# A vision tower on one NeuronCore: where the layer weights are loaded and fused, and the order in which slices, peaks, planes and gates stand in the plan

## Chip, cores, metric

The kernel runs on one core of one Trainium2 chip. The metric is the device time of one execution in microseconds (us), as the median of the runs of one kernel on one chip.

## What is computed

The reference, cut to its steps, with B = 64 images of 12 channels and 224 x 224 pixels, 196 tokens, width 192 and 4 experts:

```python
pooled = x.reshape(B, 12, 14, 16, 14, 16).sum(axis=(3, 5))
h = einsum('bcij,ce->bije', pooled, channel_weights).reshape(B, 196, 192)
n = layernorm(h); Q, K, V = n@Wq.T + bq, n@Wk.T + bk, n@Wv.T + bv
h = h + softmax(Q @ K.T / sqrt(192)) @ V
x = layernorm(h); probs = softmax(x @ w_router.T)
gate, idx = top_k(swapaxes(probs, 1, 2), 98)       # each expert takes 98 of 196 tokens
y = layernorm(x) * gamma1 + beta1
h = sum over experts of dispatch(mask(y[idx])) @ w1.T + b1
x_mlp, q, k, v = split(h)                          # 768, and 12 heads of 16
y2 = concat([gelu(x_mlp), softmax(q @ k.T / 4) @ v])
z = sum over experts of gate * mask(y2[idx] @ w2.T + b2)
out = h_tokens + x + z[..., :192] + z[..., 192:]
```

## The kernel before

Since the tokens are linear in 12 channel sums, the first attention works on 12 to 14 numbers per token, and U = 104 columns carry what the experts chose. The 64 images are taken in 8 groups of 8.

**Pooling.** Per pair of images, three tiles of x of 1568 KB (`xt`, three buffers, `fetch` issues the next load from the ACT queue, L1109) are summed by DVE in 7 slices (`pool`, L1256), GpSimd spreads them (`own_row`, L1576), TensorE turns them (`planes`, L830), ACT copies, TensorE makes token values (`tok`, L840), DVE copies (L1269). A group has four such pairs (m = 0 to 3).

**Routing** of a group, a chain: `take`, `norm1_scale`, `norm1`, first attention (`first_max`, `first_exp`, `first_mix`), `stream` to `stream_norm`, then `gate_scale` (L1354), a power on GpSimd (L1585, about 2.9 us), `gate_logits` (L1360), again a power, `gates` (L1373), `gate_rows` (L920, L1385), 13 rounds of `choose` on DVE (L1393, L1398), `chosen` (L928, L1411), `spread` (L1421), and `turn_u` (L936).

**Second attention and MLP** of an image: `project` (L968, low halves on DVE at L1445), through a scratch in DRAM to `stack`, `peak` (a score block, L986, whose row maximum DVE takes at L1456), `shift` (the 12 maxima turned at L995, copied by ACT, sent by a small DMA from SP, L730, as one more row of `qs`), `score` (L1005, exponential at L1205), `mix` (L1020), `hidden` (L956, GELU at L1183), `fc2` (L1051). `score` of heads 0 to 5 waits for the first shift row, of heads 6 to 11 for the second.

**The order** is a plan written by hand. `body` gives a group 8 x 12 slots (image, head), each with the peak of the next image's head, the score of this one, and what `fill`, `routing`, `choosing`, `turning` and `pooling` put there; every engine runs the same list in order. The plan ends with the `opening` of the next group: 8 steps with one `hidden` each, the twelve peaks of its image 0, and the tail of the last image. In pass g the slots also hold the routing of group g + 1 from slot `TAKE` on, the last pair of group g + 1, and pairs 0 to 2 of group g + 2. The sections are `prologue` (all of group 0 up to its opening, and pairs 0 to 2 of group 1), six passes `loop`, then `pen` (no pairs for a group after the next) and `last`. A slot of a plan is a place in the list, not a time.

**Setup.** SP loads the attention weights, `G` and small vectors, then w1 and w2 (L688 to L692, 2.4 MB), tile 3, and, once ACT has copied `Vp`, the product of channel and value weights, out of PSUM (L1077), a DMA that puts it into rows 12 to 23 of `G` (L696). DVE waits for this DMA before it centres `G` (L1520). `fuse` turns w1 and w2 (L814) and multiplies them into `M` (L821, L823) in three parts, at slots inside the pooling of pairs 1 to 3; part 0 on DVE adds the halves of w2 (L1264). The line that places them, and the four PSUM buffers:

```python
front += [(pieces * (m + 1) + 4, ("fuse", 0, m)) for m in range(3)]
MISC = 4
```

In the opening `hidden` and `project` share these four buffers; a buffer that held q or k is free when DVE has taken its low half (L1450).

## Time and profile before

| | before |
|---|---|
| median of 3 runs | 1775.73 us (1774.58 to 1777.63) |
| the profiled execution | 1772.98 us, its span 1771.2 us |
| TensorE matmuls (PE) | 1519.9 us, 86% of the span |
| VectorE (DVE) | 1218.1 us, 69% |
| ScalarE (ACT) | 848.6 us, 48% |
| GpSimd (POOL) | 249.4 us, 14% |
| mean granted TensorE clock | 0.921 |
| first score of groups 0 to 7, at | 231.8, 437.2, 637.5, 839.0, 1040.1, 1242.6, 1447.8, 1629.2 us |

The profiled execution is 2.75 us below the median. Spans are in us from the first instruction. PEclk is the granted TensorE clock, 1.00 for 2.4 GHz and 0.50 for 1.2 GHz. A loop pass takes 200 to 205 us, six of them make up two thirds of the span.

### The profile page before, as it was taken

The numbers are of one execution on the slowest core, as the hardware profiler recorded it, in microseconds if no ns is written. First come the engines' busy times: TensorE is split into PE (matmuls) and PEld (weight loads), VectorE is DVE, ScalarE is ACT, GpSimd is POOL, SyncE is SP. The second block draws the span as 40 slices with busy tenths as digits, with TensorE's granted clock in tenths as the row PEclk, the third lists the DMA queues.
The fourth block names the chain that finished last, engine by engine and source line by source line (L and its number), as shares of the span: only waits on it lengthen the run. The fifth ranks groups of instructions, "written<-read, shape, count | busy, mean of one in ns | idle before, by whom it ended". The sixth has DMA issues, their size and how long they took to land.

```text
span 1771.2 us, 34644 instructions
## 1 busy us (share of the span) xinstructions
PE 1519.9 (86%) x12440; PEld 1260.6 (71%) x12440; DVE 1218.1 (69%) x2822; ACT 848.6 (48%) x1935; POOL 249.4 (14%) x318
## 2 busy tenths in 40 slices
PE   1364689998998899989998899999899889989998
PEld 1233567777786777778787777778677778878786
DVE  3847678766887578865887568875787567563552
ACT  0101355545554555545654554545554555546654
POOL 2012002200121002200121002210022002110000
PEclk9757689989999999999999989989998899989999
DMA  9867376706573357606664356615656151102220
GB/s 225 233 166 195 89 179 158 188 15 161 148 187 99 85 148 178 184 16 158 156 168 117 76 145 168 180 40 136 165 149 148 35 145 45 42 19 59 50 53 15
DMA packets 99598, 218.03 MB, mean 123 GB/s; under 512 B 61371, under 2 KB 75877, under 8 KB 88678
## 3 DMA queue, kind: packets, MB, share of 16 engines
q10 hardware_dynamic: 11904, 149.33, 31.3%
q1 hardware_dynamic: 87526, 66.49, 16.5%
q8 instruction: 102, 1.67, 0.4%
q14 instruction: 66, 0.54, 0.1%
HBM read 186.57 MB, written 28.90 MB: 122 GB/s over the span
## 4 chain that ended last, share of the span: by engine, by line
PE 50%; DVE 25%; issue 13%; DMA 5%; POOL 3%; ACT 2%; SPq 1%; DVEq 0%; ACTq 0%; POOLq 0%
PE bank L1051 13%; DVE psums L1256 10%; DVE peaks L1456 6%; PE bank L956 6%; PE bank L986 5%; PE bank L1020 5%; PE bank L1005 4%; DMA qs<-shiftT 3%; POOL var L1585 3%; PE bank L968 2%; PE bank L879 2%; PE bank L830 2%; PE bank L1029 2%; PE bank L943 2%; DVE qk L1445 1%
## 5 line engine op out<-in xcount | busy, mean ns | idle before, releaser
L1456 DVE TENSOR_REDUCE peaks<-bank 98x2 f32<-98x392 f32 x768 | 423.6, 563 | 170.3 <-PE bank L986 149.3
L1205 ACT ACTIVATE Pb<-bank 98x392 f32<-98x392 f32 x768 | 374.9, 497 | 300.1 <-PE bank L1005 250.9
L1256 DVE TENSOR_REDUCE psums<-xt 112x2 f32<-112x512 f32 x672 | 425.7, 677 | 27.1 <-DVE peaks L1456 9.7
L1051 PE MATMUL bank<-w2T,hid 128*98 128x192 f32 x1536 | 311.4, 342 | 0.0
L986 PE MATMUL bank<-ks,qs 96*98 96x196 f16 x1536 | 268.4, 261 | 42.8 <-DVE peaks L1456 37.9
L1005 PE MATMUL bank<-qs,ks 97*98 97x196 f16 x1536 | 268.3, 258 | 22.1 <-DMA qs<-shiftT 20.2
L986 PEld LDWEIGHTS bank<-ks,qs 96*98 96x98 f16 x1536 | 165.5, 128 | 132.7 <-DVE peaks L1456 66.2
L1051 PEld LDWEIGHTS bank<-w2T,hid 128*98 128x98 f32 x1536 | 249.5, 176 | 3.5
L1005 PEld LDWEIGHTS bank<-qs,ks 97*98 97x98 f16 x1536 | 167.3, 130 | 34.5 <-DMA qs<-shiftT 22.9
L1020 PE MATMUL bank<-Pb,vals 98*32 98x196 f32 x3072 | 171.9, 342 | 1.2 <-ACT Pb L1205 1.2
L1613 POOL TENSOR_TENSOR fin<-fin,both 98x384 f32<-98x384 f32 x64 | 63.9, 999 | 732.9 <-DVE fin L1481 732.9
L956 PE MATMUL bank<-UT,M 104*128 104x196 f32 x768 | 150.8, 347 | 16.9 <-DVEq L1450 16.9
L956 PEld LDWEIGHTS bank<-UT,M 104*128 104x128 f32 x768 | 133.7, 200 | 21.8 <-DVEq L1450 19.3
L1183 ACT ACTIVATE hid<-bank 128x392 f32<-128x392 f32 x192 | 93.5, 497 | 109.9 <-PE bank L956 109.7
L1445 DVE TENSOR_TENSOR qk<-bank,qk 96x392 f16<-96x392 f32 x128 | 71.7, 560 | 84.6 <-ACT qk L1192 74.6
L1576 POOL TENSOR_TENSOR spread_p<-psums,cst 112x196 f32<-112x196 f32 x96 | 50.0, 521 | 533.2 <-DVE psums L1256 533.2
L1020 PEld LDWEIGHTS bank<-Pb,vals 98*32 98x32 f32 x3072 | 81.3, 110 | 54.2 <-issue 25.0
L1117 ACT COPY oT<-bank 128x196 f32<-128x196 f32 x192 | 61.9, 322 | 106.8 <-PE bank L1020 102.4
L1051 PE MATMUL bank<-w2T,onT 96*98 96x192 f32 (+1 forms) x512 | 108.3, 334 | 0.0
L968 PE MATMUL bank<-UT,M 104*96 104x196 f32 x512 | 99.0, 337 | 0.1
L830 PE MATMUL bank<-spread_p,cst 112*24 112x196 f32 x192 | 44.4, 376 | 48.8 <-POOL spread_p L1576 43.3
L1585 POOL TENSOR_TENSOR var<-var,cst 98x16 f32<-98x16 f32 x24 | 69.7, 2904 | 106.7 <-DVE var L1289 58.7
(183 smaller groups left out, 1783.6 us busy)
## 6 DMA issues: line engine op xcount, KB each, us to landing
xt<-in_x_dram ACTq DMA_DIRECT2D x93, 1568.0 KB, 9.0
qk_scratch<-qk SPq DMA_DIRECT2D x64, 294.0 KB, 4.1
qs<-qk_scratch SPq DMA_DIRECT2D x192, 73.5 KB, 3.0
ks<-qk_scratch SPq DMA_DIRECT2D x192, 73.5 KB, 3.1
out_dram<-fin SPq DMA_DIRECT2D x64, 147.0 KB
xt<-in_x_dram SPq DMA_DIRECT2D x3, 1568.0 KB, 8.8
qs<-shiftT SPq DMA_DIRECT2D x128, 2.3 KB
hid<-in_L_ffn_w_dram SPq DMA_DIRECT2D x1, 1440.0 KB
```

The source lines that it names most:

```text
L956: mm = pe.matmul(ps[:, T * j:T * j + T], M[:, 128 * f:128 * f + 128], UT[:, i, :], start=True, stop=True)
L968: mm = pe.matmul(ps[0:DC, T * c:T * c + T], M[:, f:f + DC], UT[:, i, :], start=True, stop=True)
L986: mm = pe.matmul(peak_ps[s][0:HT, T * q:T * q + T], qs[0:KS, i % NSTACK, h, HT * q:HT * q + HT], ks[0:KS, i % NSTACK, h, :], start=True, s ...
L1005: mm = pe.matmul(score_ps[s][0:HT, T * k:T * k + T], ks[:, i % NSTACK, h, HT * k:HT * k + HT], qs[:, i % NSTACK, h, :], start=True, stop=True)
L1020: mm = pe.matmul(ps[32 * j:32 * j + 32, 0:T], vals[:, i % 2, q, h, :], Pb[:, (H * i + h) % NP, q, :], start=(q == 0), stop=(q == 1))
L1051: mm = pe.matmul(misc_ps[slot][0:HT, D * h:D * h + D], lhs, w2T[0:w, f, :], start=(f == 0), stop=(f == NF + 1))
L1183: act.activation(hid[:, i, 2 * b:2 * b + 2, :].rearrange("p a b -> p (a b)"), ps[:, 0:2 * T], ACT.Gelu).then_inc(free, 1)
L1205: act.activation(Pb[:, (H * i + h) % NP, :, :].rearrange("p a b -> p (a b)"), score_ps[s][0:HT, 0:2 * T], ACT.Exp, scale=float(DH) ** -0.5 ...
L1256: last = dve.tensor_reduce(psums[:, m % 2, t, 2 * p:2 * p + 2], v[:, 2 * p:2 * p + 2, :, :], AX.XY, ALU.add)
L1445: dve.tensor_tensor(qk16[:, m, 1, :, :].rearrange("p c t -> p (c t)"), misc_ps[slot][0:DC, 0:2 * T], qk16[:, m, 0, :, :].rearrange("p c t ...
L1456: dve.tensor_reduce(peaks[:, h // 6, :, h % 6], peak_ps[s][0:HT, 0:2 * T].rearrange("p (q k) -> p q k", q=2), AX.X, ALU.max, negate=True). ...
L1585: gp.tensor_tensor(var[:, 2, :], var[:, 1, :], const("half", HT), ALU.pow).then_inc(gp_pow, 1)
```

## The change

It moves work in the plan and in the queues, and takes out one DMA; the sums and products are the same.

1. w1, w2, b1, b2 are loaded when 11 of group 0's 12 tiles are pooled. Tile 3 is fetched from the ACT queue.
2. `Vp` and its DMA are gone: `cwcT` has 25 columns, zero but for the middle 12, so that the product lands in rows 12 to 23 of PSUM and DVE adds it to `G`, which GpSimd has zeroed.
3. `fuse` 0, 1, 2 stand in group 0's routing: after `stream_norm`, between `gate_logits` and `gates`, and after the first `choose`. `L` moves into `UT`. Planes and tok of pair (1, 1) stand behind `spread`.
4. Opening: peaks of heads 0, 1 in step 2 in place of 1, and so on; 10 and 11 in step 7; the first shift in step 6, the second at the end. Slices of the opening stand ahead of its peaks. Planes and tok of the last pair there go to slots 2 and 4 of the next pass; for the two pairs before, planes stand 5 slots behind the last slice, in place of 3.5.
5. `TAKE` 23 in place of 25, `gate_logits` 3 slots behind `gate_scale` and `gates` 4 behind that (2 and 3 before); `gate_rows` stays in its slot, `chosen` comes a slot later. The slices of pair (1, 3) have 19 slots in place of 21.

```diff
 
-def routing(dg, at):
+def routing(dg, at, wide=0):
@@ -192,9 +192,9 @@
...
     at += 14
-    ops += [(at, ("gate_scale", dg)), (at + 2, ("gate_logits", dg)), (at + 5, ("gates", dg)),
-            (at + 7, ("gate_rows", dg)), (at + 7.5, ("weigh", dg))]
-    at += 8
+    ops += [(at, ("gate_scale", dg)), (at + 2 + wide / 2, ("gate_logits", dg)), (at + 5 + wide, ("gates", dg)),
+            (at + 7 + wide, ("gate_rows", dg)), (at + 7.5 + wide, ("weigh", dg))]
+    at += 8 + wide
@@ -227,16 +227,19 @@
...
-    front += [(pieces * (m + 1) + 4, ("fuse", 0, m)) for m in range(3)]
...
     front += first + [(at + 0.5 * r, ("choose", 0, r)) for r in range(ROUNDS)]
+    front += [(end + 34.5, ("fuse", 0, 0)), (at - 4.5, ("fuse", 0, 1)), (at + 0.2, ("fuse", 0, 2))]
     front += choosing(0, at + 0.5 * ROUNDS + 1)
     front += pooling(1, 0, steadily(end + 9, 0.95))
-    front += pooling(1, 1, steadily(end + 29, 0.65))
+    late = pooling(1, 1, steadily(end + 29, 0.65))
+    front += [(at + 0.5 * ROUNDS + 1.7 + 0.5 * (op[0] == "tok") if op[0] in ("planes", "tok") else slot, op)
+              for slot, op in late]
     plan = [in_order(front + turning(0, at + 0.5 * ROUNDS + 3))] + opening(0, False)
-    for slot, op in in_slots(pooling(1, 2, steadily(1, 0.24))):
-        plan[min(slot, len(plan) - 1)].append(op)
+    for slot, op in in_slots(pooling(1, AHEAD - 1, steadily(1, 0.24))):
+        if op[0] not in ("planes", "tok"):
+            plan[min(slot, len(plan) - 1)].append(op)
@@ -266,16 +269,16 @@
...
-        if 1 <= i < 7:
-            ops += [("peak", dg, 0, h) for h in range(2 * (i - 1), 2 * (i - 1) + 2)]
-        if i == 5:
+        if i >= 2:
+            ops += [("peak", dg, 0, h) for h in range(2 * (i - 2), 2 * (i - 2) + 2)]
+        if i == 6:
             ops.append(("shift", dg, 0, 0))
     ops.append(("shift", dg, 0, 1))
...
-TAKE = 25
+TAKE = 23
@@ -326,24 +329,28 @@
...
-    front, at = routing(1, TAKE)
+    front, at = routing(1, TAKE, 2)
...
     quiet = (int(at), H * GRP)
     at = rounds(plan, 1, int(at))
-    for slot, op in in_slots(choosing(1, at + 1) + turning(1, at + 4)):
+    for slot, op in in_slots(choosing(1, at + 2) + turning(1, at + 4.5)):
         plan[slot].append(op)
...
     at = evenly(plan, pieces * (GRP // PAIR - AHEAD), 0, TAKE - 4)
-    front = []
+    front = [(2, ("planes", 1, AHEAD - 1)), (4, ("tok", 1, AHEAD - 1))]
...
         at = evenly(plan, pieces * AHEAD, TAKE + 1, len(plan) - 3, quiet)
         for m in range(AHEAD):
-            front += pooling(2, m, at[pieces * m:])
+            front += pooling(2, m, at[pieces * m:], behind=5)
     for slot, op in in_slots(front):
-        plan[min(slot, len(plan) - 1)].append(op)
+        if op[0] in ("planes", "tok") and op[1:] == (2, AHEAD - 1):
+            continue
+        into = plan[min(slot, len(plan) - 1)]
+        peaks_at = [k for k, other in enumerate(into) if other[0] == "peak"]
+        into.insert(peaks_at[0] if slot >= H * GRP and peaks_at else len(into), op)
     return sum(plan, [])
@@ -517,7 +524,6 @@
...
-        cwcT = sb("cwcT", [DC, 2, C])
+        cwcT = sb("cwcT", [DC, 2, Z])
...
-        L = P1[0:DC, :, :, :].rearrange("p a b c -> p (a b c)")[:, 0:2 * U].rearrange("p (c e z) -> p c e z", c=2, e=E)
+        L = UT[0:DC, :, :].rearrange("p i t -> p (i t)")[:, 3 * 2 * D:3 * 2 * D + 2 * U].rearrange("p (c e z) -> p c e z", c=2, e=E)
...
         turns.append(([(wr_in[:, DC * c:DC * c + DC], E * c, E, DC) for c in range(2)],
...
+                      cwcT[:, :, C:2 * C]))
@@ -674,29 +680,27 @@
...
-            sp.dma_start(G[0:C, :], cw).then_inc(w_in, 16)
-            sp.dma_start(G[2 * C:Z, :], bv.rearrange("(a d) -> a d", a=1)).then_inc(w_in, 16)
...
                         .then_inc(w_in, 16)
+            sp.wait_ge(g_zero, 1)
+            sp.dma_start(G[0:C, :], cw).then_inc(w_in, 16)
+            sp.dma_start(G[2 * C:Z, :], bv.rearrange("(a d) -> a d", a=1)).then_inc(w_in, 16)
...
+            for t in range(NX + 1, NX + SETUP_TILES):
+                sp.wait_ge(pooled, t - NX + 1)
+                sp.dma_start(xt[:, t % NX, :], x_tile(0, t)).then_inc(x_in[t % NX], 16)
+            sp.wait_ge(pooled, TILES * GRP // PAIR - 1)
             sp.dma_start(w1_in[:, 0:10, :], w1[0:1280, :].rearrange("(f p) d -> p f d", p=128)).then_inc(w12_in, 16)
...
             sp.dma_start(b2_in[:, 0:2, :], b2.rearrange("(a o f) -> a o f", a=1, o=2)).then_inc(w12_in, 16)
-            sp.wait_ge(pooled, 1)
-            sp.dma_start(xt[:, 0, :], x_tile(0, NX)).then_inc(x_in[0], 16)
-            sp.wait_ge(su_act, 2)
-            sp.dma_start(G[C:2 * C, :], Vp).then_inc(su_dma, 16)
-            for t in range(NX + 1, NX + SETUP_TILES):
-                sp.wait_ge(pooled, t - NX + 1)
-                sp.dma_start(xt[:, t % NX, :], x_tile(0, t)).then_inc(x_in[t % NX], 16)
@@ -756,11 +760,11 @@
...
                     for d in range(2):
-                        mm = pe.matmul(banks[1][0:C, 0:D], cwcT[:, d, :], wa_T[:, 2, d, :],
+                        mm = pe.matmul(banks[1][0:Z, 0:D], cwcT[:, d, :], wa_T[:, 2, d, :],
@@ -1068,17 +1072,20 @@
             act.wait_ge(w_in, 16 * W_LOADS)
             for t in range(1, NX):
                 act.dma_start(xt[:, t, :], x_tile(0, t)).then_inc(x_in[t], 16)
+            act.wait_ge(pooled, 1)
+            act.dma_start(xt[:, 0, :], x_tile(0, NX)).then_inc(x_in[0], 16)
             for n_, (parts, dst) in enumerate(turns):
                 if n_ == NT - 1:
                     act.wait_ge(su_pe, 1)
...
-                    act.wait_ge(su_pe, 2)
-                    act.copy(Vp, banks[1][0:C, 0:D]).then_inc(su_act, 1)
@@ -1494,6 +1501,7 @@
...
+            dve.memset(cwcT[:, :, :], 0.0)
@@ -1516,7 +1524,8 @@
...
-            dve.wait_ge(su_dma, 16)
+            dve.wait_ge(su_pe, 2)
+            done(dve.tensor_tensor(G, G, banks[1][0:Z, 0:D], ALU.add))
@@ -1562,6 +1571,7 @@
...
+            gp.memset(G, 0.0).then_inc(g_zero, 1)
```

Left out are the plain consequences (a semaphore for the zeroed `G`, counts of waits).

**Group 0's choosing rounds, PE.** Before (`L920` gate rows, `L830` and `L840` the pair (1, 1), `L928` the choice turned):

```order
55 L912 MATMUL bank<-WR,zT 98x148 x2
56 L920 MATMUL bank<-cst,prob 32x98 x2
57 L830 MATMUL bank<-spread_p,cst 24x196 x3
58 L840 MATMUL bank<-WI,planesT 98x48 x2
59 L928 MATMUL bank<-cst,rows 98x32 x2
```

With the change (`L818` the turns of w1 and w2, `L924` gate rows, `L825` and `L827` the products into `M`):

```order
46 L818 MATMUL bank<-cst,both 128x96 x12
47 L818 MATMUL bank<-cst,both 96x96 x4
48 L924 MATMUL bank<-cst,prob 32x98 x2
49 L825 MATMUL bank<-hid,UT 104x384 x2
50 L827 MATMUL bank<-M,cst 104x384
...
55 L825 MATMUL bank<-hid,UT 104x192 x2
56 L827 MATMUL bank<-M,cst 104x192
57 L932 MATMUL bank<-cst,rows 98x32 x2
58 L834 MATMUL bank<-spread_p,cst 24x196 x3
59 L844 MATMUL bank<-WI,planesT 98x48 x2
```

The products stand between gate rows and the choice, the pair behind it.

**The opening in a loop pass, ACT.** Before (`L1183` GELUs, three to an image, `L1109` fetches, `L1117` copies of shift row and planes):

```order
238 L1109 DMA xt<-in_x_dram 112x3584
239 L1183 ACTIVATE hid<-bank 128x392 x3
240 L1117 CAST shiftT<-bank 6x196
241 L1183 ACTIVATE hid<-bank 128x392 x3
242 L1109 DMA xt<-in_x_dram 112x3584
243 L1183 ACTIVATE hid<-bank 128x392 x3
244 L1117 CAST shiftT<-bank 6x196
245 L1117 COPY planesT<-bank 24x196
```

With the change (lines are 7 higher):

```order
242 L1116 DMA xt<-in_x_dram 112x3584
243 L1190 ACTIVATE hid<-bank 128x392 x6
244 L1116 DMA xt<-in_x_dram 112x3584
245 L1124 CAST shiftT<-bank 6x196
246 L1190 ACTIVATE hid<-bank 128x392 x3
247 L1124 CAST shiftT<-bank 6x196
```

The first shift row stood six GELUs ahead of the planes' copy and ahead of the last fetch; it now stands right behind that fetch.

**The same opening, DVE.** Before (`L1456` peaks, `L1256` slices, `L1445` low halves), then with the change (`L1463`, `L1263`, `L1452`):

```order
648 L1456 TENSOR_REDUCE peaks<-bank 98x2 x2
649 L1256 TENSOR_REDUCE psums<-xt 112x2 x2
650 L1456 TENSOR_REDUCE peaks<-bank 98x2 x2
651 L1256 TENSOR_REDUCE psums<-xt 112x2 x5
652 L1445 TENSOR_TENSOR qk<-bank,qk 96x392 x2
```

```order
646 L1263 TENSOR_REDUCE psums<-xt 112x2 x7
647 L1463 TENSOR_REDUCE peaks<-bank 98x2 x2
648 L1452 TENSOR_TENSOR qk<-bank,qk 96x392 x2
649 L1263 TENSOR_REDUCE psums<-xt 112x2 x4
650 L1463 TENSOR_REDUCE peaks<-bank 98x2 x2
```

Five slices stood ahead of the low halves; now two peaks do.

## Rows read from the trace of the kernel before

**Rows 1.** Busy time by stretch, one loop period: us, then busy per engine, PEclk, DMA share, GB/s
```profile
783.00:984.00 201.00, 184.18 (x1540) 154.12 (x1540) 149.61 (x348) 104.67 (x240) 29.63 (x39) 0.95 0.52 133
```

**Rows 2.** Timeline of DVE, start of the program: start us, length, line, idle before and its releaser
```profile
42.36 0.34 DVE L1520 TENSOR_REDUCE mean<-hid 25x1 f32<-25x192 f32 x1 [26.91 <-DMA hid<-hid]
...
83.64 4.24 DVE L1256 TENSOR_REDUCE psums<-xt 112x2 f32<-112x512 f32 x7 [2.57 <-DMA xt<-in_x_dram]
89.93 4.24 DVE L1256 TENSOR_REDUCE psums<-xt 112x2 f32<-112x512 f32 x7 [2.04 <-DMA xt<-in_x_dram]
...
106.86 0.26 DVE L1269 COPY tok_raw<-bank 98x96 f32<-98x96 f32 x1 [9.71 <-PE bank L840]
107.04 7.20 DVE L1256 TENSOR_REDUCE psums<-xt 112x2 f32<-112x512 f32 x12
...
118.79 0.26 DVE L1276 COPY wtok<-tok_raw 98x192 f32<-98x192 f32 x1
```

**Rows 3.** DMA issues of the page, tiles of x: count, KB each, us to landing
```profile
xt<-in_x_dram ACTq DMA_DIRECT2D x93, 1568.0 KB, 9.0
```

**Rows 4.** Busy time by stretch, at the start
```profile
20.00:30.00 10.00, 2.23 (x10) 1.15 (x9) 0.00 (x0) 0.50 (x2) 0.00 (x0) 1.00 1.05 269
...
90.00:100.00 10.00, 10.00 (x16) 3.35 (x15) 5.45 (x9) 0.31 (x1) 0.52 (x1) 0.50 0.74 209
```

**Rows 5.** Timeline of DVE at the start, the sum of the two halves of w2
```profile
58.47 2.14 DVE L1264 TENSOR_TENSOR both<-hid 96x1920 f32<-96x1920 f32 x1
```

**Rows 6.** Timeline of PE, group 0's fused weights and its choosing rounds
```profile
90.69 2.88 PE L821 MATMUL bank<-hid,P 96*104 96x384 f32 x4
...
106.05 0.78 PE L840 MATMUL bank<-WI,planesT 24*98 24x48 f32 x4
...
172.09 0.48 PE L920 MATMUL bank<-cst,prob 98*32 98x98 f32 x2 [12.16 <-DVEq L1380]
174.65 2.12 PE L830 MATMUL bank<-spread_p,cst 112*24 112x196 f32 x6 [2.08 <-POOL spread_p L1576]
177.27 0.86 PE L840 MATMUL bank<-WI,planesT 24*98 24x48 f32 x4 [0.49 <-ACT planesT L1117]
189.29 0.34 PE L928 MATMUL bank<-cst,rows 32*98 32x32 f32 x2 [11.16 <-issue]
```

**Rows 7.** Timeline of PE, opening of a later group
```profile
817.77 2.98 PE L956 MATMUL bank<-UT,M 104*128 104x196 f32 x8 [2.46 <-DVEq L1450]
...
836.64 1.18 PE L830 MATMUL bank<-spread_p,cst 112*24 112x196 f32 x6
...
838.96 0.33 PE L1005 MATMUL bank<-qs,ks 97*98 97x196 f16 x2
```

**Rows 8.** Busy time by stretch, around that opening's stall and after the gates
```profile
750.00:756.00 6.00, 6.00 (x26) 5.40 (x26) 4.21 (x12) 0.99 (x2) 1.92 (x1) 0.51 0.73 154
...
815.00:824.00 9.00, 6.54 (x22) 5.76 (x22) 3.22 (x6) 1.66 (x4) 0.52 (x1) 0.63 0.54 139
```

**Rows 9.** Timeline of PE, image 5 of the same loop pass
```profile
742.69 0.37 PE L1005 MATMUL bank<-qs,ks 97*98 97x196 f16 x2 [1.69 <-DMA qs<-shiftT]
...
747.68 1.16 PE L830 MATMUL bank<-spread_p,cst 112*24 112x196 f32 x6 [2.10 <-POOL spread_p L1576]
```

**Rows 10.** Timeline of POOL, the same place
```profile
744.14 2.91 POOL L1585 TENSOR_TENSOR var<-var,cst 98x16 f32<-98x16 f32 x1 [4.75 <-DVE var L1354]
```

**Rows 11.** Timeline of ACT, two issues of a tile of x
```profile
734.30 0.32 ACTq L1109 DMA_DIRECT2D xt<-in_x_dram  x1
...
833.00 0.32 ACTq L1109 DMA_DIRECT2D xt<-in_x_dram  x1
```

**Rows 12.** Timeline of SP, a shift row's issue
```profile
735.38 0.68 SPq L730 DMA_DIRECT2D qs<-shiftT  x1
```

**Rows 13.** Timeline of PE, before the choice of rows is turned
```profile
785.99 0.25 PE L928 MATMUL bank<-cst,rows 32*98 32x32 f32 x2 [3.11 <-issue]
```

**Rows 14.** Timeline of PE, group 6, before its gates
```profile
1546.73 0.37 PE L986 MATMUL bank<-ks,qs 96*98 96x196 f16 x2 [1.37 <-DVE peaks L1456]
```

More of the change, by code:

```diff
@@ L519, in bass_vit_tower @@
         Gc = scratch(Z, D)
-        Vp = scratch(C, D)
         w2_sum = both[0:DC, 0:2 * (HID + D)] \
@@ L550, in bass_vit_tower @@
         turn_full, turn_free = sem("turn_full"), sem("turn_free")
-        su_dve, su_pe, su_act, su_dma = sem("su_dve"), sem("su_pe"), sem("su_act"), sem("su_dma")
+        su_dve, su_pe, su_act, g_zero = sem("su_dve"), sem("su_pe"), sem("su_act"), sem("g_zero")
         bias_in = sem("bias_in")
@@ L648, in bass_vit_tower @@
         turns.append(([(cwc[:, DC * c:DC * c + DC], C * c, C, DC) for c in range(2)],
-                      cwcT[:, :, :].rearrange("p c e -> p (c e)")))
+                      cwcT[:, :, C:2 * C]))
         turns.append(([(Gc[:, DC * c:DC * c + DC], Z * c, Z, DC) for c in range(2)],
@@ L758, in _ @@
                                 mm = pe.matmul(banks[0][0:DC, 12 * (2 * m + c):12 * (2 * m + c) + 12],
-                                               wa_T[:, m, d, DC * c:DC * c + DC], cwcT[:, d, :],
+                                               wa_T[:, m, d, DC * c:DC * c + DC], cwcT[:, d, C:2 * C],
                                                start=(d == 0), stop=(d == 1))
@@ L948, in hidden @@
                 if at.section == "pro":
-                    pe.wait_ge(su_act, 3)
+                    pe.wait_ge(su_act, 2)
                     pe.wait_ge(bias_in, 16)
@@ L961, in project @@
                 if at.section == "pro":
-                    pe.wait_ge(su_act, 3)
+                    pe.wait_ge(su_act, 2)
                 pe.wait_ge(UT_ready, GRP * G_ + i + 1)
@@ L1080, in _ @@
                 cols = parts[-1][1] + parts[-1][2]
-                act.copy(dst, misc_ps[n_ % MISC][0:rows_, 0:cols]).then_inc(turn_free, 1)
+                src = misc_ps[n_ % MISC][0:rows_, 0:cols]
+                if len(dst.shape) == 3:
+                    src = src.rearrange("p (c e) -> p c e", c=2)
+                act.copy(dst, src).then_inc(turn_free, 1)
             def fuse(at, G_, dg, part):
```

## The prediction

> **What bounds the kernel now.** I read the busy time of a loop period first, then the timelines. Over one period of 201 us PE is busy 184.18 us and DVE 149.61 us [rows 1]: TensorE carries the time, and what a pass can lose is its 16.8 us idle and what it does at half rate. So the loop's price is read at each place where PE waits, and the start, where DVE and the loads set the pace, is read apart.
>
> At the start DVE stands still for 26.91 us until a 9 KB DMA lands [rows 2]: it is queued with 2.4 MB of w1 and w2, and between 20 and 30 us the DMA engines are full although no slice runs [rows 4]. Later slices wait for tiles that come 6.29 us apart (83.64 to 89.93), then 9.71 us for a `tok` that sits behind the products into `M`, and the last slice ends at 107.04 + 7.20 = 114.24 [rows 2].
>
> In a loop pass there are four larger waits. (a) In the opening PE waits 2.46 us for DVE's low halves of image 2 [rows 7], which stand behind five slices; after it the clock is down (0.63 granted over 9 us, so 6.7 us at 1.2 GHz) [rows 8]. (b) At image 5, 1.69 us for a shift row, whose DMA was issued right behind a tile of x. (c) Then 2.10 us for a spread slice [rows 9] that GpSimd does behind the 2.91 us power of the gates [rows 10]; here too 6 us at half rate follow, PE being busy for all of it [rows 8]. (d) 3.11 us before the choice [rows 13], where DVE ends its rounds.
>
> **The start, step by step.** The DMA into `G` and its wait go; DVE goes on when the product is in PSUM, about 22 us. Tile 1 is issued at 14.6 as before, and a tile takes 9.0 us to land [rows 3]: 23.6. Ten more at 6.2 us (nearest: 6.29) put tile 11 at 85.6; its slices end 4.24 us later, at 89.8 [rows 2]. That is 24.4 us before 114.24. The ends: 26 if tiles come 6.0 us apart; 15 if the 2.4 MB, released when tile 10 is pooled, go wholly ahead of tile 11 (about 9 us at the 269 GB/s of [rows 4]). I take 24.4, since tile 11 is then all but landed.
>
> Moved into the routing: the addition of w2's halves, 2.14 us [rows 5] and 0.3 us for b2's, stands on DVE in a stretch where DVE has slices back to back: +2.4 us on the path. The turns of w1 and w2 fall into PE's 12.16 us of idle before gate rows [rows 6]: nothing, and about 2 us if that cover were gone. The products took from 90.69 to 106.05, 15.4 us, at half rate although PE was busy all the time [rows 4, 6]. They now start at gate rows and must end by the choice: 189.29 - 172.09 = 17.2 us [rows 6]. They just fit: nothing, and 1 to 3 us late if copies or the choice are earlier. Planes and tok of pair (1, 1), 177.27 + 0.86 - 174.65 = 3.5 us [rows 6], move out of that cover behind `spread`, whose 2.1 us and PE's own 3.0 us of waiting cover all but 0.5. Group 0's opening I leave as it is: its slices still stand behind the peaks. Start: 24.4 - 2.4 - 0.5 = **21.5 us** gained.
>
> **The loop, per pass.**
> - Opening, the stall (a). Two peaks stand ahead of the low halves now, not five slices: 2.46 us gone, and with it 6.7 us at half rate, of which 6.3 busy: 3.1 us. Back comes a wait of peaks 6, 7 behind the last slices and `gate8` on DVE, 0.8 us by their durations. So the last fetch, behind the GELUs of image 6, is issued at 833.00 - 4.8 = 828.2 [rows 11].
> - The shift row. It is now sent right behind this fetch. At (b) the same happened: fetch 734.30, shift row 735.38, score 742.69, that is 8.39 us from the fetch to the score [rows 9, 11, 12]. So the first score comes at 828.2 + 8.4 = 836.6, where it came at 838.96 [rows 7]: 2.4 us gained of the 4.8 plus the 2.1 us of planes and tok that left (836.64 to the next peak). PE would be there at about 832.3 and waits some 4 us.
> - Planes and tok come back in slots 2 and 4 of the next pass, 1.18 us [rows 7] and about 0.5: -1.6. DVE has two more slices in the first image: -0.3.
> - Gates (c). The power starts two slots earlier against PE's planes, and 3 slots are more than its 2.91 us: 2.10 us of wait and half of 6 us at the low clock: **5.1 us**, the largest term. Bounds: 0 if the spread is still late, 5.1.
> - Waits for shift rows. The fetch ahead of (b) stands a slot earlier: +1.3 of 1.69. Two fetches now stand a slot ahead of second shift rows (images 3 and 4), where none did: up to -1.69 each by the same row; slots there are long, I take -1.0 in all.
> - Choice (d). PE has one slot more of work in front of it: +0.9 of 3.11.
>
> Sum: 2.4 - 1.6 - 0.3 + 5.1 + 1.3 - 1.0 + 0.9 = **6.8 us** a pass, 41 us in six. In `pen` the power delays the peaks by 1.37 us [rows 14]: 1.4 + 0.9 = 2.3.
>
> The profiled execution is 1772.98 us: 1772.98 - 21.5 - 41 - 2.3 = 1708. The median of the runs is 2.75 us higher, so I forecast **1711 us**, against 1775.73.
>
> The shift row is where a page rule is weighed. The row shows a small DMA, alone in its queue, that releases PE 8.39 us after the tile's issue, about when a tile lands [rows 3, 9, 11]. The Trainium skill (DMA: Bandwidth & Descriptors, Queues, rings and completion order) says the semaphore increment "lands only after every earlier write from that SDMA engine, across its queues", which speaks against this change; the trace agrees at (b). The same section says that an engine takes turns between its queues packet by packet; by that alone the row would overtake the tile, and rival 1 below would hold.
>
> **Rivals.**
> 1. *The small DMA is early.* The first score then starts when PE is there, 832.3 and not 836.6: 4.3 us more a pass, 26 in all, 1685. For it: the fetch could slip behind the shift row if ACT's GELUs run late. Against: (b) shows 8.39 us, and the order on ACT puts the fetch first.
> 2. *The loop keeps its waits under other names.* The planes no longer wait for GpSimd, but the clock is still down after the shift wait or after DVE's peaks, and the first image, with DVE and PE both nearly full, pays 2 us. Then a pass gains 2.3: 1773.0 - 21.5 - 14 - 1 = 1736.5, as a median 1739. For it: a pass has many small waits on peaks, and each could grow when its neighbour shrinks. Against: PE is idle 16.8 us of 201 [rows 1] and the two stalls are single events with a cause.
> 3. *The start gives little,* because w1 and w2 hold up the tiles after all or the products do not fit under the choosing rounds: 10 us in place of 21.5, 1722.
> 4. *Slower: the opening's shift wait.* Place: the first score of each pass. If (a) stays, the fetch is at 833.0 and lands after 9.8 us: score at 842.8, 3.9 us late. The idle PE then runs 6 us at half rate (3.0), planes and tok cost 1.6, the two new neighbours 3.4, and only 5.1 + 1.3 + 0.9 come in: 4.6 us lost a pass. With 27.6 lost in six and 23.8 gained elsewhere: 1777 against 1773, 1780 as a median. It decides from about 4 us a pass. For it: a wait of about 4 us is sure in my own sum. Against: it needs (a) too, which five slices in front of one low half made. The skill's page on TensorE (TensorE: Matmul & The Clock Gate, What's actually happening) says that idleness returns the array to half rate and activity lifts it; (c) shows both.
>
> **How the numbers follow.** Forecast 0.50, rival 1 0.15, rival 2 0.24, rival 3 0.06, rival 4 0.05. The forecast's own range is 1698 to 1725: 4 us of the start, 1.5 us a pass. Range: rival 1's 1688 as a median below, rival 2's 1739 above. A difference of 0.2% (3.5 us) is about what a measurement can tell. Faster: 0.94, all but rival 4 and a rest; within 0.2%: 0.02; slower: 0.04.
>
> **What would show it.** Start: DVE never waits over 10 us before 90 us, and `take` is near 94 us (118.79 before [rows 2]). The products run from about 151 to 166 and the choice does not wait for them. Opening: no wait for L1450's successor, and a wait of some 4 us of the first score for the shift row; if there is none, rival 1. Gates: planes of pair (2, 1) without a wait, 1.00 granted behind them. Choice: a wait near 2.2 us. Period of a pass: 194 to 195 us. Were passes above 199 us, or `take` later than 104 us, the prediction would be wrong.

## The result, and the profile after

| | before | changed |
|---|---|---|
| median (20 runs each) | 1776.72 us | 1788.03 us (1775.39 to 1797.99) |
| profiled execution, span | 1772.98, 1771.2 us | 1784.52, 1782.7 us |
| mean granted TensorE clock | 0.921 | 0.935 |
| first score of groups 0 to 7 | 231.8 ... 1629.2 | 218.7, 422.9, 625.1, 832.9, 1037.9, 1243.1, 1450.6, 1639.5 |

The ratio is 1.0059, 95% interval 1.0041 to 1.0077: slower, where 1711 us were forecast. Medians here and below leave out two slow runs of e3 and two of e7, more than 1.5% above the fastest of their kernel. Group 0 is 13.1 us ahead at its first score; group 7 is 10.3 us behind. So the six loop passes and `pen` lose 23.4 us where they should have gained 43: the six passes lose 15.9 (41 forecast as gain), `pen` 7.5 (2.3). A pass takes 202.2 to 207.9 us, above the 199 that the prediction named as a sign of being wrong.

Busy time by stretch, changed kernel: one pass, the stretch around the first score (832.94) and its wait, the one around the wait for `x_tok`, and the place of the gates. Columns are as in [rows 1]:

```profile
832.94:1037.90 204.96, 183.73 (x1541) 155.24 (x1541) 149.63 (x348) 104.99 (x239) 29.65 (x39) 0.94 0.51 131
...
830.50:837.50 7.00, 4.56 (x22) 3.03 (x23) 1.74 (x4) 1.80 (x4) 0.00 (x0) 0.52 0.32 80
874.70:881.50 6.80, 6.16 (x25) 5.63 (x26) 5.04 (x12) 1.64 (x4) 0.83 (x2) 0.50 0.30 69
...
950.00:956.00 6.00, 5.05 (x43) 3.54 (x36) 4.67 (x17) 2.46 (x7) 4.51 (x3) 1.00 1.00 270
```

PE is as busy as in [rows 1] (183.73 us against 184.18), and 21.2 us idle against 16.8. By image (first score to first score, the pass of group 3; the last column is the stretch from the last score to the next group's first):

| | 0 | 1 | 2 | 3 | 4 | 5 | 6 | 7 | opening |
|---|---|---|---|---|---|---|---|---|---|
| before | 12.6 | 20.5 | 21.8 | 23.7 | 26.1 | 23.2 | 15.8 | 18.7 | 38.7 |
| changed | 14.0 | 21.8 | 27.2 | 26.6 | 24.7 | 19.9 | 17.1 | 17.3 | 36.4 |

The opening and image 5, at which the change aims, are shorter. Images 2 and 3 are together 8.3 us longer; the prediction has nothing for image 2 and a part of 1.0 us for image 3. PE there and at the marks that the prediction named, changed kernel, timeline:

```profile
832.94 0.56 PE L1009 MATMUL bank<-qs,ks 97*98 97x196 f16 x2 [4.38 <-DMA qs<-shiftT]
...
875.34 0.56 PE L852 MATMUL bank<-cst,x_tok 98*128 98x98 f32 x2 [2.46 <-DVE x_tok L1305]
...
908.81 0.55 PE L1009 MATMUL bank<-qs,ks 97*98 97x196 f16 x2 [1.93 <-DMA qs<-shiftT]
...
951.97 1.16 PE L834 MATMUL bank<-spread_p,cst 112*24 112x196 f32 x6 [0.39 <-POOL spread_p L1586]
...
987.84 0.25 PE L932 MATMUL bank<-cst,rows 32*98 32x32 f32 x2 [0.78 <-issue]
991.21 0.35 PE L940 MATMUL bank<-cst,both 98*104 98x98 f32 x2 [1.34 <-DVE both L1428]
```

The stall at the low halves [rows 7] is gone, the planes no longer wait [rows 9], the choice waits 0.78 us [rows 13] but the turns behind it 1.34. In their place stand 4.38 us for the shift row and two waits that were not there: 2.46 us for `x_tok`, 1.93 us for image 3's second shift row. `x_tok` is late because of norm1's power (POOL, then DVE):

```profile
871.56 2.91 POOL L1595 TENSOR_TENSOR var<-var,cst 98x16 f32<-98x16 f32 x1 [6.25 <-DVE var L1296]
```

```profile
874.50 0.36 DVE L1301 TENSOR_TENSOR a_tok<-z_tok,var 98x192 f32<-98x192 f32 x1 [0.96 <-POOL var L1595]
874.90 0.29 DVE L1305 COPY x_tok<-a_tok 98x256 f32<-98x256 f32 x1
```

DVE waited for the power before the change too, even longer (1.31 us, against 0.96 here), but PE did not notice: it had two pieces of `fc2`, a residual and a `mix` in front of the same turn while the power ran; with TAKE 23 the turn stands ahead of them. The kernel before, PE's timeline there:

```profile
876.37 1.14 PE L1051 MATMUL bank<-w2T,hid 128*98 128x192 f32 x6
...
878.01 1.14 PE L1051 MATMUL bank<-w2T,hid 128*98 128x192 f32 x6
...
880.07 0.87 PE L1020 MATMUL bank<-Pb,vals 98*32 98x196 f32 x16
880.96 0.36 PE L848 MATMUL bank<-cst,x_tok 98*128 98x98 f32 x2
```

DVE at the start, changed kernel:

```profile
24.41 4.24 DVE L1263 TENSOR_REDUCE psums<-xt 112x2 f32<-112x512 f32 x7 [0.70 <-DMA xt<-in_x_dram]
...
73.71 4.24 DVE L1263 TENSOR_REDUCE psums<-xt 112x2 f32<-112x512 f32 x7 [2.35 <-DMA xt<-in_x_dram]
80.31 4.24 DVE L1263 TENSOR_REDUCE psums<-xt 112x2 f32<-112x512 f32 x7 [2.35 <-DMA xt<-in_x_dram]
...
93.43 4.24 DVE L1263 TENSOR_REDUCE psums<-xt 112x2 f32<-112x512 f32 x7 [2.10 <-DMA xt<-in_x_dram]
...
102.22 0.26 DVE L1283 COPY wtok<-tok_raw 98x192 f32<-98x192 f32 x1
```

The 26.91 us wait [rows 2] is gone and `take` is 16.6 us earlier; ten tiles took 69.0 us, 6.9 each.

### The profile page after: what moved, and what is told of

The parts are those of the page before. It is cut to its first block, busy times and chain, and to the rows that moved or that the text cites. A ratio compares the mean times of both kernels' runs of the same rounds, so it can differ in the third digit from the quotient of the medians.

```text
span 1782.7 us, 34638 instructions
## 1 busy us (share of the span) xinstructions
PE 1516.6 (85%) x12440; PEld 1267.3 (71%) x12440; DVE 1217.3 (68%) x2824; ACT 849.2 (48%) x1934; POOL 249.6 (14%) x319
## 4 chain that ended last, share of the span: by engine, by line
PE 52%; DVE 19%; issue 12%; DMA 10%; POOL 3%; ACT 3%; SPq 0%; DVEq 0%; ACTq 0%; POOLq 0%
PE bank L1055 14%; DMA qs<-shiftT 6%; PE bank L960 6%; DVE psums L1263 5%; PE bank L990 5%; PE bank L1024 4%; PE bank L1009 4%; DVE peaks L1463 4%; DMA xt<-in_x_dram 4%; PE bank L972 3%; POOL var L1595 3%; PE bank L883 2%; PE bank L834 2%; PE bank L1033 2%; DVE qk L1452 2%
## 5 line engine op out<-in xcount | busy, mean ns | idle before, releaser
L1463 DVE TENSOR_REDUCE peaks<-bank 98x2 f32<-98x392 f32 x768 | 422.8, 562 | 208.5 <-PE bank L990 191.7
L1263 DVE TENSOR_REDUCE psums<-xt 112x2 f32<-112x512 f32 x672 | 426.7, 678 | 45.3 <-DMA xt<-in_x_dram 22.7
L990 PE MATMUL bank<-ks,qs 96*98 96x196 f16 x1536 | 272.8, 265 | 54.6 <-DVE peaks L1463 53.1
L1009 PE MATMUL bank<-qs,ks 97*98 97x196 f16 x1536 | 271.9, 261 | 39.3 <-DMA qs<-shiftT 38.1
L990 PEld LDWEIGHTS bank<-ks,qs 96*98 96x98 f16 x1536 | 171.2, 131 | 144.2 <-DVE peaks L1463 79.5
L1623 POOL TENSOR_TENSOR fin<-fin,both 98x384 f32<-98x384 f32 x64 | 63.9, 998 | 668.3 <-DVE fin L1488 668.3
L960 PE MATMUL bank<-UT,M 104*128 104x196 f32 x768 | 144.3, 337 | 1.2 <-DVEq L1457 1.2
L960 PEld LDWEIGHTS bank<-UT,M 104*128 104x128 f32 x768 | 128.7, 193 | 6.6 <-DVEq L1457 3.3
L1452 DVE TENSOR_TENSOR qk<-bank,qk 96x392 f16<-96x392 f32 x128 | 71.8, 561 | 82.7 <-ACT qk L1199 73.0
L834 PE MATMUL bank<-spread_p,cst 112*24 112x196 f32 x192 | 49.7, 410 | 58.4 <-POOL spread_p L1586 51.6
L1615 POOL TENSOR_SCALAR tm<-tT,cst 128x196 f32<-128x196 f32 x128 | 54.5, 431 | 223.0 <-ACT tT L1124 125.4
```

The source lines that it names most:

```text
L834: mm = pe.matmul(ps[0:PAIR * C, 0:T], const("plane", PP)[:, PAIR * C * t:PAIR * C * t + PAIR * C], spread_p[:, t, :, :].rearrange("p a b - ...
L960: mm = pe.matmul(ps[:, T * j:T * j + T], M[:, 128 * f:128 * f + 128], UT[:, i, :], start=True, stop=True)
L990: mm = pe.matmul(peak_ps[s][0:HT, T * q:T * q + T], qs[0:KS, i % NSTACK, h, HT * q:HT * q + HT], ks[0:KS, i % NSTACK, h, :], start=True, s ...
L1009: mm = pe.matmul(score_ps[s][0:HT, T * k:T * k + T], ks[:, i % NSTACK, h, HT * k:HT * k + HT], qs[:, i % NSTACK, h, :], start=True, stop=True)
L1263: last = dve.tensor_reduce(psums[:, m % 2, t, 2 * p:2 * p + 2], v[:, 2 * p:2 * p + 2, :, :], AX.XY, ALU.add)
L1452: dve.tensor_tensor(qk16[:, m, 1, :, :].rearrange("p c t -> p (c t)"), misc_ps[slot][0:DC, 0:2 * T], qk16[:, m, 0, :, :].rearrange("p c t ...
```

## The experiments

Theories at the outset: **A**, TAKE 23 moved norm1's power and a fetch to places where PE pays; **B**, the new opening costs more than it gives; **C**, the start's gain is eaten later. The kernel before, timed beside them on the same chips, had medians from 1774.6 to 1778.4 us. e1, e4, e9 and so on are the labels' first parts.

| run | what | median us | ratio to before, interval |
|---|---|---|---|
| e1 | before + start | 1758.2 | 0.990 [0.987, 0.993] |
| e2 | changed, TAKE 25 | 1768.1 | 0.996 [0.993, 0.998] |
| e3 | changed, opening's last fetch later | 1769.6 | 0.997 [0.993, 1.000] |
| e4 | before + opening | 1789.4 | 1.007 [1.004, 1.009] |
| e5 | changed, norm1 later | 1774.6 | 1.002 [0.999, 1.004] |
| e6 | changed, narrow gates | 1802.3 | 1.017 [1.014, 1.021] |
| e7 | changed, old opening | 1783.2 | 1.005 [1.002, 1.008] |
| e8 | e5 + e7 | 1770.9 | 0.998 [0.995, 1.000] |
| e9 | e1 + TAKE 23 | 1820.5 | 1.024 [1.021, 1.028] |
| e10 | e1, TAKE 24, gates 1 wider, norm1 later | 1752.8 | 0.987 [0.985, 0.990] |
| e11 | e1, three fetches moved | 1778.2 | 1.002 [0.999, 1.004] |
| e12 | e11, slices behind low halves | 1769.5 | 0.997 [0.994, 0.999] |
| e13 | changed, one fetch moved | 1764.3 | 0.992 [0.990, 0.994] |
| e14 | e10, slices as e12, later planes | 1744.2 | 0.979 [0.975, 0.983] |
| e15 | changed, planes early again | 1821.8 | 1.026 [1.024, 1.028] |
| e16 | before + planes and tok deferred | 1781.4 | 1.002 [1.000, 1.004] |
| e17 | e14, one fetch moved | 1723.2 | 0.971 [0.968, 0.974] |
| e18 | e17, choice later | 1724.4 | 0.970 [0.967, 0.974] |

**e1: the start alone.** Points 1 to 3 of the change on the kernel before; body, opening, TAKE and gates untouched.

> The kernel before with the change's start alone: late loads of w1 and w2, the added product in place of the transfer, the fused weights in group 0's routing, planes and tok of pair (1, 1) behind spread; opening, loop, TAKE and gates as before. Theory A (the start's gain stays to the end): the first score of group 0 comes about 13 us earlier, at 218 to 219, and the median is 12 to 14 us under the kernel before, about 1763. Rival B (the start's gain is eaten in the first passes, which wait for tiles that the late weights pushed back): first score of group 1 less than 8 us earlier, median over 1770.

17.3 us less, more than the 12 to 14 of A, with the first score at 218.6. A holds by the medians and C falls. The profiled execution is the slowest of the six (1768.7 us) and by group 7 has kept only 4.3 of its 13 us, so the trace of e1 is no measure of the loop.

**e4 and e7: the opening, alone and taken back.** e4 is the kernel before with point 4 of the change (without `behind=5`); e7 is the changed kernel with the old lines, planes and tok of the last pair in the opening again:

```diff
-        if i >= 2:
-            ops += [("peak", dg, 0, h) for h in range(2 * (i - 2), 2 * (i - 2) + 2)]
-        if i == 6:
+        if 1 <= i < 7:
+            ops += [("peak", dg, 0, h) for h in range(2 * (i - 1), 2 * (i - 1) + 2)]
+        if i == 5:
...
-        into.insert(peaks_at[0] if slot >= H * GRP and peaks_at else len(into), op)
+        plan[min(slot, len(plan) - 1)].append(op)
```

> The kernel before with the change's opening alone: peaks and shift rows a step later, slices in front of peaks, planes and tok of the last pair in slots 2 and 4 of the next pass; start, TAKE, gates as before. Theory A (the shift row's wait takes the place of the stall at the low halves, and its slow stretch too): the stretch from the last score to the first is about 2 us shorter, images 0 and 1 together 2 to 3 us longer: 0 to 1 us a pass, median within 6 us of the kernel before, 1773 to 1783. Rival B (my forecast's sum, in which the opening gains 0.5 us a pass with no slow stretch behind the wait): 1773, with no half rate behind the first score. Rival C (the stall at the low halves stays and the shift wait comes on top): over 1795.

> The changed kernel with the opening of before: peaks and shift rows a step earlier, slices behind the peaks of their step, planes and tok of the last pair in the opening. Theory A (the new opening costs what it cost alone, 14 us): no wait of 4 us at the first score, the stall at the low halves back, 1774. Theory B (my forecast's sum: the new opening gains about 0.5 us a pass): 1791.

Alone it costs 13.9 us. e4's profiled execution is 17.6 us longer than that of the kernel before: 3.6 of them are there at group 0's first score, and 8.1 come in one pass, in which a tile took 13.5 us to land and image 1's second shift row was waited for 5.23 us. Within the changed kernel the new opening costs 4.8 us by the medians and 1.4 by the ratios, which is not clear of zero. So B holds alone and does not explain the result.

**e16: planes and tok alone.**

```diff
-    front = []
+    front = [(2, ("planes", 1, AHEAD - 1)), (4, ("tok", 1, AHEAD - 1))]
```

> The kernel before with nothing changed but planes and tok of the last pair, which stand in slots 2 and 4 of the next pass. It splits the new opening's 14 us (e4). Theory A (their work is only moved, and the first shift row lands later than PE comes): the wait at the first score grows from 0 to about 1 us, 0 to 1 us a pass, 1773 to 1781. Theory B (the first image is so tight on DVE and PE that they cost their whole 1.6 us and some half rate there): 1785 to 1790, all of e4's loss.

3 us, not clear of zero. The rest of e4's loss came with the order of peaks, slices and shift rows, or is scatter of single passes such as the one above; these were not split further.

**e2, e9, e5: TAKE.** e2 is the changed kernel with 25 for 23, e9 is e1 with 23 for 25; e5 moves norm1 within the changed kernel's routing:

```diff
-TAKE = 23
+TAKE = 25
```

```diff
-           (at + 3.5, ("norm1", dg)), (at + 4.5, ("norm1_turn", dg)), (at + 5.5, ("norm1_key", dg))
+           (at + 5, ("norm1", dg)), (at + 5.5, ("norm1_turn", dg)), (at + 6, ("norm1_key", dg))
```

> The changed kernel with TAKE at 25 again, gates still 2 slots wider. Theory A (routing that begins two slots earlier puts the power of norm1 where PE has too little to do beside it: 2.46 us of wait at x_tok and up to 6.8 us at half rate behind it): that wait goes, with its slow stretch, about 5 us in each of seven passes, 35 in all: about 1753. Rival B (the passes are longer by the denser slices and the waits for shift rows, and the norm1 wait only stands where another would): within 8 us of the changed kernel, 1780 to 1790.

> The change's start and, of everything else, TAKE 23 alone (gates, opening, planes as before). Base is e1, 1758. Theory A (TAKE 23 is the change's costly part: the wait at x_tok, the fetch in front of image 3's second shift row, the gates' exponential on ACT waited for): images 2 and 3 take 53 us a pass where e1 takes 45.5, image 5 gains nothing; 1785 to 1800. Rival B (TAKE 23 costs only together with the wider gates or the new opening): under 1770.

> The changed kernel with TAKE at 23, but norm1 and its two turns later inside the routing: norm1 4 slots behind norm1_scale in place of 2.5. By the slice schedule one fetch also slips from slot 38 to 39, behind the second shift row of image 3. Theory A (the two slots moved norm1's power out of its cover): no wait of 2.46 us at x_tok, no slow stretch behind it; and no wait of 1.9 us for the shift row at image 3: 5 to 8 us in each of seven passes, about 1748. Rival B (DVE is what is late there, not the power): x_tok still waited for, over 1775.

TAKE 23 alone costs 62 us, one and a half times the most that I expected. e9, PE's timeline in the pass of group 3:

```profile
900.97 0.56 PE L847 MATMUL bank<-cst,x_tok 98*128 98x98 f32 x2 [2.46 <-DVE x_tok L1300]
...
935.10 0.56 PE L1004 MATMUL bank<-qs,ks 97*98 97x196 f16 x2 [2.77 <-DMA qs<-shiftT]
...
979.56 2.12 PE L829 MATMUL bank<-spread_p,cst 112*24 112x196 f32 x6 [4.37 <-POOL spread_p L1581]
```

Three waits: the two new ones, and the planes' wait of [rows 9] grown from 2.10 to 4.37 us, since the power starts two slots earlier against the same planes. The six loop passes, first score of group 0 to that of group 6, in e9 and then in the kernel before, whose loop is that of e1:

```profile
222.70:1492.30 1269.60, 1145.25 (x9240) 960.18 (x9241) 901.39 (x2087) 629.66 (x1434) 177.94 (x234) 0.91 0.50 127
```

```profile
231.80:1447.80 1216.00, 1112.80 (x9240) 929.79 (x9241) 899.39 (x2087) 628.74 (x1434) 177.82 (x234) 0.94 0.52 133
```

The loop is 53.6 us longer: 21.2 more of PE idle, and 32.4 more of PE busy with the same 9240 matmuls at a lower granted clock (0.91 against 0.94). As a mean of the six passes, image 2 (`x_tok`) is 5.3 us longer, image 3 (the shift row, with the fetch of slot 38 ahead of it) 5.9, images 5 and 6 (the planes) 5.6, and the rest 8 shorter. So norm1's power is one of three parts of about the same size.

e5 takes 0.8 us off the first wait (2.46 to 1.65) and shortens image 2 by 2.3 us a pass: 13.4 us in all, where theory A had 40. What is left of the wait is not the power: in e5 DVE starts on `a_tok` at 870.45 without a wait, 0.94 us after the power's end, straight behind two peaks and two `on_tok`. So rival B holds for the rest. Its fetch, now 0.09 us behind the shift row, did not help: the row took 8.5 us, with 2.21 us of wait at slot 42. e2 gains 20 us: images 2 and 3 are 5.2 and 4.5 us shorter a pass, the opening 8.2 longer. That choice and turns come two slots later with wide gates is the likely reason, not shown; e2, PE in the opening:

```profile
987.25 1.67 PE L960 MATMUL bank<-UT,M 104*128 104x196 f32 x4 [3.20 <-DVEq L1457]
```

**e8: e5's edit and e7's together.**

> Both of the above: old opening and late norm1, that is the change's start, TAKE 23 and wider gates without its two costs. If the costs add: e5's result less e7's gain of 14 us, about 1735, 40 us under the kernel before. If the two hide each other, no better than the better of e5 and e7.

The costs do not add: 17 us under the changed kernel, 3.7 better than e5, where the sum had 1735.

**e6 and e15: the gates' two parts.**

```diff
-    front, at = routing(1, TAKE, 2)
+    front, at = routing(1, TAKE)
```

```diff
-            front += pooling(2, m, at[pieces * m:], behind=5)
+            front += pooling(2, m, at[pieces * m:])
```

> The changed kernel with gate_logits 2 and gates 3 slots behind their predecessors, as before (the choice comes two slots earlier with them). Theory A (my forecast's term, 5.1 us a pass for wider gates): the wait of 2.2 us for a spread slice at the planes of pair (2, 1) is back with 6 us at half rate: 1788 + 31 = 1819. Theory B (the trace of the changed kernel: images 5 and 6 together are only 2.0 us shorter than before, since other waits took the place): about 1800. Theory C (spreading the gates is worth nothing, because the same slots are only moved): 1780 to 1792.

> The changed kernel with planes 3.5 slots behind the last slice as before, gates still wide. It splits the gates' part with e6 (wide taken back: 1802). Theory A (the later planes do the work: PE meets GpSimd's spread behind the power again): 1805 to 1820. Theory B (the wider gates do it, the planes' place is free): 1785 to 1792.

Taken back one at a time in the changed kernel, the wider gates are worth 14.3 us, the later planes 33.8; both with the choice, from e9 to e7, are worth 37.3, so the two are not to be added. e15, PE and POOL:

```profile
968.74 1.15 PE L834 MATMUL bank<-spread_p,cst 112*24 112x196 f32 x3 [4.38 <-POOL spread_p L1586]
```

```profile
965.20 2.90 POOL L1595 TENSOR_TENSOR var<-var,cst 98x16 f32<-98x16 f32 x1 [1.81 <-DVE var L1361]
968.08 0.52 POOL L1586 TENSOR_TENSOR spread_p<-psums,cst 112x196 f32<-112x196 f32 x1
```

The spread slice stands behind the whole power. In e6 the planes are late enough, but ACT waits 3.26 us for the gates' inputs from DVE and PE 2.47 us for an `oT` that ACT has behind it.

**e3, e11, e13, e17: fetches and shift rows.** Each moves fetches in the plan: e3 the opening's last one to the end, e13 the fetch of slot 38 to 41, e11 those of slots 12, 56, 62 to 16, 58, 64, e17 that of slot 12 to 17 (and e14's other edits):

```diff
+        if op == ("fetch", 2, AHEAD - 1, TILES - 1):
+            plan[-1].append(op)
+            continue
```

```diff
+    late = {("fetch", 2, 0, 1): 40.9}
+    front = [(late.get(op, slot), op) for slot, op in front]
```

e11 and e17 have the second form, with `{("fetch", 1, 3, 0): 15.9, ("fetch", 2, 1, 1): 57.9, ("fetch", 2, 1, 2): 63.9}` and `("fetch", 1, 3, 0): 16.9`.

> The changed kernel with one fetch moved: the opening's last tile of x is issued behind both shift rows, not in front of the first. Theory A (the small DMA lands with the tile that is issued 0.8 us before it): the shift row lands in 1.7 us, the first score's wait of 4.4 us goes and with it some 2 us of half rate, 6.5 us in each of the six openings: 39 us, about 1749. Rival B (the wait is for something else, such as the row's own copy or its second half): the wait stays above 3 us, time within 5 us of the changed kernel. Rival C (the tile then comes late for the next pass): waits of DVE for a tile in image 0 or 1, half of the 39 us given back.

> The change's start (e1), with three fetches of the loop moved behind a shift row: slot 12 to 16, 56 to 58, 62 to 64. Theory A (a small row lands with the tile that is in flight beside it): the waits for shift rows at slots 18 (0.7 to 5 us) and 60 (1 to 1.5 us) go, 3 us a pass: about 1740. Rival B (the rows are late for another reason): the waits stay, 1758. Rival C (the later tiles stop DVE, which then stops PE): new waits of DVE for tiles and no gain.

> The changed kernel with one fetch a pass moved from slot 38, ahead of image 3's second shift row, to slot 41, two slots behind it (where it stood before the change). Theory A (a shift row that is sent within a few tenths of a microsecond of a tile lands with the tile, one sent 2 us ahead of it does not): the wait of 1.9 us at slot 42 and the half rate behind it go, about 3 us in each of six passes: 1770. Rival B (only the x_tok wait ahead of it brings the clock down, and the row's wait is idle time that comes back later): within 5 us of 1788.

> As e14 (1744.2), with the first fetch of pair (1, 3) in slot 17 in place of 12: two slots behind image 1's second shift row (in e11 it stood in slot 16, sent 0.1 us behind the row, which then landed 8.5 us late with it). Theory A (about 2 us ahead of the tile is enough): no wait at slot 18, 1 us in a usual pass and 7 in the one pass that loses 7.4 there: 12 us less, 1732. Rival B (the tile then is still in flight at image 2's first row, slot 21, and the wait goes there): 1740 to 1748.

One fetch moved (e13) is worth 23.7 us, 4 a pass, twice its wait; image 3 is 3.8 us shorter by the traces. e11 is a miss: 20 us slower than e1. Its issues, SP, ACT and then PE:

```profile
857.25 0.70 SPq L731 DMA_DIRECT2D qs<-shiftT  x1
```

```profile
857.37 0.32 ACTq L1113 DMA_DIRECT2D xt<-in_x_dram  x1
```

```profile
867.79 0.56 PE L1006 MATMUL bank<-qs,ks 97*98 97x196 f16 x2 [5.19 <-DMA qs<-shiftT]
```

The row went out 0.12 us ahead of the tile and PE had it only at 867.79. In e13 it went out 1.46 us ahead, and in e17, at the same place as in e11, 0.95 us ahead:

```profile
894.25 0.70 SPq L736 DMA_DIRECT2D qs<-shiftT  x1
```

```profile
895.71 0.32 ACTq L1118 DMA_DIRECT2D xt<-in_x_dram  x1
```

```profile
828.04 0.70 SPq L731 DMA_DIRECT2D qs<-shiftT  x1
```

```profile
828.99 0.32 ACTq L1113 DMA_DIRECT2D xt<-in_x_dram  x1
```

By the semaphore's last event these two rows landed 1.7 us after their issue, e11's 10.5 us (8.5 to 10.5 in its six passes).

e17 is 21 us under e14 by the medians, 15 by the ratios to the kernel before. The traces do not account for that: image 1 is 1.1 us a pass shorter, image 2 1.0 longer, with 0.96 us of wait at its first row. In e3 the first score's wait is gone, but the row for heads 6 to 11, sent 0.1 us ahead of the moved tile, took 8.3 us, and the half rate stayed. e3, by stretch behind its first score:

```profile
829.50:839.70 10.20, 9.38 (x50) 6.09 (x51) 4.68 (x10) 4.69 (x12) 0.00 (x0) 0.50 0.75 187
```

So 18 of the 39 us that theory A promised came: the opening is 4.4 us a pass shorter than in the changed kernel, image 0 3.0 longer. What brings the clock down there is open: it fell without the 4 us wait.

**e10, e12, e14, e18: what is left put together.** e10 is e1 with `TAKE = 24`, `routing(1, TAKE, 1)` and e5's edit; e12 is e11, e14 is e10, each with this, e14 also with `behind=5`:

```diff
+    late = {("pool", 2, 2, 1, 4): 99, ("pool", 2, 2, 1, 5): 99, ("pool", 2, 2, 1, 6): 99, ("pool", 2, 2, 2, 3): 100}
+    front = [(late.get(op, slot), op) for slot, op in front]
```

> The change's start with TAKE 24, gates wider by one slot only, and norm1 4 slots behind norm1_scale; choice and opening in the slots of before. Theory A (the gates need cover, and norm1 too, and both can have it): no wait over 1 us at x_tok, the planes of pair (2, 1) wait less than 1 us; 2 us a pass under e1, about 1746. Rival B (one slot is too little for the 2.9 us power): the wait of 2.2 us with 6 us at half rate stays, 1755 to 1765.

> As e11, and in the loop's opening three slices go from step 2 to step 3 and one from step 3 to step 4, so that two slices and not five stand ahead of the low halves of image 2. Theory A (those five slices made the stall): the 2.46 us wait falls under 1 us and its half rate with it, 4 to 5 us in six openings under e11: about 1715. Rival B (the stall moves to peaks 6 to 9, behind the slices): 2 us or less a pass, 1730 to 1740.

> As e10 (1752.8), with the slices of e12's opening and planes 5 slots behind the last slice as in the change. Theory A (what is left of the change's good parts adds up): stall of the opening 0.7 in place of 2.5 us, 8 us as between e11 and e12, and the wait of 2.5 us at slot 61 with some 8 us at half rate gone or under 1 us, 4 us a pass: about 1722. Rival B (a new wait of ACT for the gates' exponential takes the place of the planes' wait, as in e6): only the 8 us, 1745.

> As e17, with the choice and the turns behind it in the slots of the change (choice one slot later, turns half a slot). Theory A (my forecast's term, 0.9 us a pass): the wait before the choice falls from 2.15 to under 1 us: 6 us under e17. Rival B (the turns then wait for DVE's masks, 1.3 us as in the changed kernel): within 3 us of e17.

e10's `x_tok` wait is 0.40 us, its planes still wait 2.54, and at 5.4 us under e1 it lies between A and B. e12 cuts the opening's stall from 2.46 to 0.68 us, but DVE is late at a peak instead (0.72 to 1.73 us): 8.7 us under e11, rival B. e14 has the planes' wait at 0.50, and rival B's time, not A's 1722. e18's choice waits 0.79 us in place of 2.14, its turns 1.35: nothing gained. e17 at 1723.2 us beats both kernels, that before by 2.9% and the changed one by some 3.5%. One pass of its profiled execution, the slowest of its six (1738.6 us), by stretch:

```profile
812.30:1009.70 197.40, 183.68 (x1542) 154.20 (x1541) 149.00 (x349) 104.44 (x240) 29.57 (x39) 0.95 0.54 136
```

PE's busy time is that of before and of the change; its idle time is 13.7 us, against 16.8 before and 21.2 in the change.

## Why the prediction was wrong, step by step

By medians the change adds up so: start -17.3 (e1), TAKE 23 +62.3 (e9), wide gates with later planes and choice -37.3 (e9 to e7), opening +4.8 (e7 to the changed kernel): +12.5, measured +11.3. The parts depend on the order in which they are put in: TAKE 23 costs 62 us beside narrow gates and early planes, 20 us in the changed kernel (e2).

- **The missing step: TAKE 23.** Of the earlier routing I priced the gates' slots and the fetches, never norm1's power, though it is the same 2.9 us operation whose cover I weighed at the gates. The wait for `x_tok` behind it, the planes' wait that doubles with an earlier power, and the fetch ahead of image 3's second shift row make up the 62 us, with the half rate behind them. This turns the sign: with TAKE 25 the changed kernel is 7.4 us under the kernel before (e2). It is not the whole miss, since e2 still lies 57 us above the forecast.
- **"5.1 us, the largest term"** for the gates. The wait of 2.1 us fell to 0.39 and its half rate did go, and the slot is at 1.00 (last row of the stretches above). Images 5 and 6 together are only 2.0 us shorter in that pass. I credited slots; most of it is the later planes, 33.8 us, which had no term of their own, and it repairs mostly what TAKE 23 made worse (4.38 us, not 2.10).
- **"I take -1.0 in all"** for the two fetches ahead of second shift rows: one of them cost 4.0 us a pass (e13). The wait of 1.93 us is near (b)'s 1.69, and as much again came behind it. The row of (b) had the price of its wait; that "slots there are long" was no row.
- **The opening.** Fetch 824.13, first score 832.94: 8.8 us where I had 8.4, and a wait of 4.38 where I had about 4: right. The opening is 2.3 us shorter in that pass (2.4 forecast), image 0 1.4 longer (1.9). No half rate was charged to the wait, though the clock stood at 0.52 for 7 us around it; rival 4 charged it. The loss that e4 shows alone, 13.9 us, was in no term.
- **The start, "ten more at 6.2 us"**: 6.9, hence `take` at 102.22 and not 94. With this same start the seventeen profiled executions (their openings differ) have their first score between 211.0 and 223.9 us; in the earliest `take` is at 96.5. The products fitted as worked out (gate rows 157.43, choice 174.58, wait 1.42 us); 3.5 us of the 16.6 were lost again by the first score, 1.9 of them ahead of the choice.
- **The choice**, +0.9 of 3.11: the wait fell further than forecast and came back at the turns (e18): 0.78 us where I had about 2.2, and 1.34 at the turns, which I had at nothing.
- **Rivals.** Rival 1 is out: the row waits for the tile. Rival 2 had the kind of the error, waits under other names, and 28 of the 77 us. Rival 4 had the sign from the wrong place. In the range, 1688 to 1739, no case had a moved chain that loses its cover.

## What to carry to other kernels

When a chain of steps is moved by a few slots, list every wait that it hides, not those that the move is meant to cure: each power on GpSimd was covered by the matmuls that happened to stand behind it. Count a small DMA by what is in flight with it, and send it about 1 us ahead of a large transfer, not just ahead (0.95 us was enough here, 0.12 was not). Take a change of several parts apart on the chip: the start was good, one number in the plan cost three and a half times what the start gave when it was put in alone, and about as much as it beside the other parts.
